# Expert layer of an audio tower: eight hidden buffers, products issued four experts at a time, and a new order of router and normalisation

## The chip, the cores and the metric

The kernel runs on one core of a Trainium2 chip. The time is that of one execution on the device, in microseconds (us).
## What is computed

The program is an audio tower of five blocks on 64 tiles of 128 tokens with 64 channels, in float32. The change touches the third block, the first layer of experts, a mixture of 16 experts in which each token uses the best two:

```python
gate_logits = x @ gate_w + gate_b
topk_vals, topk_idx = jax.lax.top_k(gate_logits, K)          # K = 2 of E = 16
topk_w = jax.nn.softmax(topk_vals, axis=-1)
h = jax.nn.relu(jnp.einsum('bsh,ehf->bsef', x, w1) + b1)     # 64 -> 128
expert_out = jnp.einsum('bsef,efh->bseh', h, w2) + b2        # 128 -> 64
sel = jnp.take_along_axis(expert_out, topk_idx[:, :, :, None], axis=2)
moe = jnp.sum(topk_w[..., None] * sel, axis=2)
y = x + moe
mu = jnp.mean(y, axis=-1, keepdims=True)
var = jnp.var(y, axis=-1, keepdims=True)
return (y - mu) / jnp.sqrt(var + EPS) * gamma + beta
```

Its x is the normalised output of the stage ahead, and its result is added to that output (`h`).

## The kernel before

`experts0` computes all 16 experts for every token and weighs the results, with weight 0 for the 14 that were not chosen. The tokens go in 16 groups (`TG`) of four tiles (512 tokens); two buffers `b` alternate. Two experts are a unit `n` (eight units, `NE`). Each engine has a program of its own for a group; nothing but the order written there and the semaphores sets the order of the work.

For a unit, TensorE's `hidden(n)` makes the 8 passes of the first product (L1320) into one of two pairs of PSUM banks (n even or odd); ScalarE applies a Relu for each of the two experts (L1496) into one of four buffers `hid`; TensorE's `out(n)` makes the 32 passes of the second product (L1332) into one of two banks; VectorE multiplies them with the tokens' weights into `part` (L1454); GpSimd adds `part` to the sum `acc` (L1282). `hidden(n)` must wait until the Relus of unit n-2 have read its banks. `Step.at(r, k)` is the value that a semaphore has after k events of round r.

Work for the next group g+1 is woven between the units of group g:

- the turn: GpSimd normalises g+1, TensorE transposes it (`T.pe`, L690), ScalarE copies it out (`T.act`, L697, into `xs`);
- the router: `logits` on TensorE (L1302), then on VectorE the logits (L1413), the best two by MAX8 and FIND_INDEX8, and the `gap` of the two (L1427); ScalarE takes its exponential (L1482), VectorE the two weights (`soften`), GpSimd the weights by expert (`weigh`);
- for the present group: TensorE transposes the weights (L1349), ScalarE copies them (`wT`, L1504), TensorE multiplies them with the experts' second biases (L1356), VectorE adds the input (`base`, L1461), and at the group's end `y` is the folded sum plus `base`.

The group before is normalised meanwhile (`finish`): statistics, variance, square root on ScalarE (L1489), and the result into `h`. Exp and Sqrt each need a table load on ScalarE, since they alternate. Groups 2 to 13 run in a hardware loop of two groups a turn, whose waits are computed in registers; groups 0, 1, 14 and 15 are written out. In the loop the table load for Exp stands behind the wait for `gap`; in the part written out it stands ahead of it.

In TensorE's order before, `hidden` runs one unit ahead: hidden(0), then for each n hidden(n+1), out(n). The turn of g+1 comes behind out(1), the logits of g+1 ahead of out(4). ScalarE does the turned copy behind the Relu of expert 7, Exp behind that of expert 13.

Of the kernel before, what the change touches and what calls it, by code (L numbers as in the profile page):

```python
# [17 lines left out]
ALU = mybir.AluOpType  # L18
# [4 lines left out]
C = 64  # L23
# [26 lines left out]
COLS += [("gatew", EXPERTS0), ("gatebr", EXPERTS0), ("iota16", EXPERTS0), ("eb1", EXPERTS0),  # L50
# [1129 lines left out]
def experts0(nc, ctx, m):  # L1180
# [18 lines left out]
    hid = [sb(f"hid{n}", [P, NT]) for n in range(4)]  # L1199
# [10 lines left out]
    yc_sb, yn_sb, h_sb, h_stat = step("yc_sb"), step("yn_sb", 2), step("h_sb"), step("h_stat", TS)  # L1210
# [9 lines left out]
    def rounds(eng, rest, ahead, finish=None):  # L1220

        def call(f, g, b):
            return lambda k: f(g, b, k) if f else None

        ahead(0, 0, None)
        rest(0, 0, call(ahead, 1, 1), call(None, 0, 0))
        rest(1, 1, call(ahead, 2, 0), call(finish, 0, 0))
        with eng.Fori(1, TG // 2 - 1) as i:
            rest(2 * i, 0, call(ahead, 2 * i + 1, 1), call(finish, 2 * i - 1, 1))  # L1230
            rest(2 * i + 1, 1, call(ahead, 2 * i + 2, 0), call(finish, 2 * i, 0))
        rest(TG - 2, 0, call(ahead, TG - 1, 1), call(finish, TG - 3, 1))
        rest(TG - 1, 1, call(None, 0, 0), call(finish, TG - 2, 0))
        for k in range(E if finish else 0):
            finish(TG - 1, 1, k)

    def pool(eng):
        def ahead(g, b, k):
            if k in (0, None):
                T.pool(eng, g, b)  # L1240

                sl = bass.ds(g * TS, TS)
                eng.wait_ge(T.norm_sb.sem, T.norm_sb.at(g, 1))
                settle(eng, m)
                eng.tensor_tensor(m.h[:, sl, :], m.h[:, sl, :], col(m, "betr").unsqueeze(1).broadcast_to([P, TS, C]),
                                  ALU.add).then_inc(beta_sb.sem, 1)

            if k in (1, None):
                weigh(g, b)

        def finish(g, b, k):

            if k == 3:
                sl = bass.ds(g * TS, TS)
                eng.wait_ge(var_sb.sem, var_sb.at(g))
                eng.wait_ge(yn_sb.sem, yn_sb.at(g - 1))
                settle(eng, m)
                eng.tensor_tensor(yc[:, :, :], m.y[:, sl, :], bc(y_mean[:, :], ALL), ALU.subtract).then_inc(yc_sb.sem, 1)
# [13 lines left out]
        def rest(g, b, ahead, finish):  # L1272
            for e in range(E):
                n = e // 2
                if e == 3:
                    eng.wait_ge(part_sb.sem, part_sb.at(g, 2))
                    eng.tensor_tensor(acc[:, :, :, :], part[0][:, :, :, :], part[1][:, :, :, :],
                                      ALU.add).then_inc(sum_sb.sem, 1)
                elif e % 2 and e > 1:
                    eng.wait_ge(part_sb.sem, part_sb.at(g, n + 1))  # L1280
                    eng.wait_ge(sum_sb.sem, sum_sb.at(g, n - 1))
                    eng.tensor_tensor(acc[:, :, :, :], acc[:, :, :, :], part[n % RING][:, :, :, :],  # L1282
                                      ALU.add).then_inc(sum_sb.sem, 1)
                finish(e)
                if e == 1:
                    ahead(0)
                if e == 14:
# [3 lines left out]
            eng.tensor_tensor(fold[:, :, :], acc[:, :, 0, :], acc[:, :, 1, :], ALU.add).then_inc(sum_sb.sem, 1)  # L1291

        eng.wait_ge(*T.norm)
        eng.memset(wT[:, :], 0.0).then_inc(zeros, 1)
        rounds(eng, rest, ahead, finish)

    def pe(eng):
        def logits(g, b):
            eng.wait_ge(T.xs_sb.sem, T.xs_sb.at(g))
            for p in range(TS // 2):  # L1300
                for r, rows in enumerate(HALVES):
                    mm = eng.matmul(m.ps[:, r, 256 + p * E:256 + (p + 1) * E], T.xs[b][rows, p * P:(p + 1) * P],  # L1302
                                    col(m, "gatew", rows), start=True, stop=True)
            mm.then_inc(logit_ps.sem, 1)

        def ahead(g, b, k):
            if k in (0, None):
                eng.wait_ge(logit_sb.sem, logit_sb.at(g - 1))
                T.pe(eng, g, b)
            if k in (1, None):  # L1310
                eng.wait_ge(base_sb.sem, base_sb.at(g - 1))
                logits(g, b)

        def rest(g, b, ahead, finish):
            def hidden(n):
                eng.wait_ge(hid_sb.sem, hid_sb.at(g, 2 * n - 2) if n >= 2 else hid_sb.at(g - 1))
                for j in range(2):
                    e = 2 * n + j
                    for r, rows in enumerate(HALVES):
                        mm = eng.matmul(m.ps[:, 2 + 2 * (n % 2) + r, j * 256:(j + 1) * 256],  # L1320
# [911 lines left out]
```

## Time and profile before

| what | value |
| --- | --- |
| median of 3 runs | 1213.65 us (1213.61 to 1213.88) |
| profiled execution | 1214.44 us, its span 1212.7 us, clock 0.939 |
| first to last product of this stage's experts | 422.6 to 786.4 us, with the norm behind it to 794.75 us |
| busy in the whole span | PE 1053.4, PEld 733.9, DVE 724.5, ACT 690.5, POOL 508.0 us |

A row of the time line gives the start (us from the span's start), the duration, the engine and line, what is written and read, how many instructions are merged in it, and in brackets how long the engine stood idle ahead of it and for whom. A row `x32` of L1332 is one unit's second product, `x8` of L1320 one unit's first product.

### The profile page before, as it was taken

The page shows a single profiled execution, that of the slowest core. Times are in us where ns is not written, and L with a number is a line of the kernel's source. Part 1 is how long each engine was busy: PE and PEld are TensorE (multiplying, and loading weights), DVE is VectorE, ACT ScalarE, POOL GpSimd, SP SyncE. Part 2 cuts the span into 40 slices and gives each one's busy share as a digit, 9 for nine tenths or more (in the row PEclk, how much of TensorE's full clock was granted, in tenths as well). Part 3 has the DMA queues.
Part 4 walks back from the last instruction along what each step waited for, and adds up shares of the span by engine and source line. Part 5 has one row for each costly group of instructions (what it writes and reads, how often), then busy time and mean ns, then how long its engine had stood idle before and what let it go on. Part 6 is the DMA issues. An engine that isn't in the chain of part 4 may idle for free.

```text
span 1212.7 us, 35394 instructions
## 1 busy us (share of the span) xinstructions
PE 1053.4 (87%) x12426; PEld 733.9 (61%) x12426; DVE 724.5 (60%) x1976; ACT 690.5 (57%) x1290; POOL 508.0 (42%) x780
## 2 busy tenths in 40 slices
PE   3698865999998798888888889969999999968998
PEld 1254444777766676666677667736666666645555
DVE  3466634677745646555655655627888888863443
ACT  1245443777754565565556556537777777744554
POOL 0000002555526455555555555534555555542110
PEclk9999986999977999899899989969999999988999
DMA  9423000000000000000000000000000000000101
GB/s 250 67 38 42 1 1 0 2 0 0 0 1 1 1 2 3 2 0 0 0 0 0 0 0 1 3 1 1 3 0 0 0 0 0 1 1 10 22 17 22
DMA packets 10769, 14.92 MB, mean 12 GB/s; under 512 B 9296, under 2 KB 9296, under 8 KB 9680
## 3 DMA queue, kind: packets, MB, share of 16 engines
q1 hardware_dynamic: 10704, 14.06, 5.5%
q8 instruction: 40, 0.66, 0.2%
q14 instruction: 25, 0.20, 0.1%
HBM read 11.96 MB, written 2.10 MB: 12 GB/s over the span
## 4 chain that ended last, share of the span: by engine, by line
PE 70%; DVE 10%; issue 10%; ACT 4%; POOL 4%; DVEq 1%; DMA 0%; ACTq 0%; SPq 0%; POOLq 0%
PE ps L1332 7%; PE ps L1320 7%; PE ps L1701 6%; PE ps L1723 5%; PE ps L1709 4%; PE ps L221 3%; PE ps L1691 3%; PE ps L1865 3%; PE ps L1898 3%; POOL e_acc L1282 3%; PE ps L1689 2%; PE ps L859 2%; PE ps L858 2%; PE ps L231 2%; DVE c_max L351 2%
## 5 line engine op out<-in xcount | busy, mean ns | idle before, releaser
L1496 ACT ACTIVATE e_hid<-ps,cst 128x512 f32<-128x512 f32 x256 | 161.3, 680 | 101.8 <-PE ps L1320 101.6
L1332 PE MATMUL ps<-ew,e_hid 128*64 128x64 f32 x4096 | 155.5, 230 | 41.1 <-ACT e_hid L1496 40.8
L1332 PEld LDWEIGHTS ps<-ew,e_hid 128*64 128x64 f32 x4096 | 136.2, 141 | 78.4 <-ACT e_hid L1496 48.3
L1282 POOL TENSOR_TENSOR e_acc<-e_acc,e_part 128x512 f32<-128x512 f32 x96 | 125.3, 1306 | 107.6 <-DVE e_part L1454 107.2
L1320 PE MATMUL ps<-e_xs,ew 64*128 64x256 f32 x1024 | 153.6, 428 | 0.0
L1454 DVE TENSOR_TENSOR e_part<-ps,e_wt 128x512 f32<-128x512 f32 x128 | 88.1, 688 | 99.0 <-PE ps L1332 95.9
L1320 PEld LDWEIGHTS ps<-e_xs,ew 64*128 64x128 f32 x1024 | 98.4, 204 | 19.7 <-issue 3.5
L1747 DVE TENSOR_REDUCE a_rmax<-ps 128x8 f32<-128x1024 f32 x64 | 78.2, 1223 | 36.0 <-PE ps L1701 34.0
L1656 POOL TENSOR_TENSOR a_sum<-a_part 128x256 f32<-128x256 f32 x64 | 46.5, 726 | 105.1 <-DVE a_part L1758 105.1
L1709 PEld LDWEIGHTS ps<-cst,a_ex 128*128 128x128 f32 x512 | 55.0, 140 | 49.7 <-issue 49.7
L204 POOL TENSOR_TENSOR t_prob<-t_ex,t_rscale 128x512 f32<-128x512 f32 x8 | 12.0, 1502 | 169.4 <-DVE t_rscale L377 169.4
L1750 DVE TENSOR_TENSOR a_diff<-ps,a_rmax 128x1024 f32<-128x1024 f32 x64 | 78.4, 1224 | 2.9
L1792 ACT ACTIVATE a_prob<-ps 128x1024 f32<-128x1024 f32 x64 | 65.6, 1024 | 20.3 <-PE ps L1709 18.7
L1701 PE MATMUL ps<-a_u,a_xs 64*128 64x512 f32 x256 | 71.5, 635 | 4.7 <-DVE a_diff L1750 4.5
L1723 PE MATMUL ps<-a_v,a_prob 128*64 128x66 f32 x2048 | 73.9, 224 | 1.1 <-DVE a_part L1758 1.1
L1723 PEld LDWEIGHTS ps<-a_v,a_prob 128*64 128x64 f32 x2048 | 65.0, 136 | 11.7 <-issue 11.7
L1709 PE MATMUL ps<-cst,a_ex 128*128 128x128 f32 x512 | 70.0, 279 | 1.7 <-ACT a_ex L1787 1.6
L221 PE MATMUL ps<-x_in,w1s 48*128 48x512 f32 x128 | 43.7, 764 | 31.1 <-DVE c_max L351 13.6
L351 DVE TENSOR_REDUCE c_max<-ps 128x128 f32<-128x1024 f32 x32 | 39.2, 1224 | 51.3 <-PE ps L221 51.3
L1787 ACT ACTIVATE a_ex<-a_diff 128x1024 f32<-128x1024 f32 x64 | 67.2, 1051 | 3.2 <-DVE a_diff L1750 2.6
L2000 ACT ACTIVATE e_hid<-ps,cst 128x512 f32<-128x512 f32 x64 | 38.8, 688 | 24.3 <-PE ps L1865 24.3
L1775 ACT ACTIVATE a_u<-ps 128x1024 f32<-128x1024 f32 x32 | 32.8, 1025 | 33.4 <-PE ps L1689 33.4
(272 smaller groups left out, 2207.4 us busy)
## 6 DMA issues: line engine op xcount, KB each, us to landing
x_in<-x_dram SPq DMA_DIRECT2D x48, 128.0 KB, 4.7
cst<-cst_dram SPq DMA_DIRECT2D x1, 2965.0 KB, 16.6
out_dram<-e_res SPq DMA_DIRECT2D x16, 128.0 KB, 2.0
ew<-ew_dram SPq DMA_DIRECT2D x1, 1024.0 KB, 18.6
cst<-cst_dram SPq DMA_DIRECT2D x1, 704.0 KB, 7.5
ew<-ew_dram SPq DMA_DIRECT2D x1, 512.0 KB, 20.3
cst<-cst_dram SPq DMA_DIRECT2D x1, 329.5 KB, 3.1
```

Of the source, the lines that this page charges most:

```text
L221: mm = eng.matmul(m.ps[:, r, :], w1s[rows, :], x_in[b][rows, h * 512:(h + 1) * 512], start=True, stop=True)
L1282: eng.tensor_tensor(acc[:, :, :, :], acc[:, :, :, :], part[n % RING][:, :, :, :], ALU.add).then_inc(sum_sb.sem, 1)
L1320: mm = eng.matmul(m.ps[:, 2 + 2 * (n % 2) + r, j * 256:(j + 1) * 256], w1[rows, e * F0:(e + 1) * F0], T.xs[b][rows, :], start=True, stop=True)
L1332: mm = eng.matmul(m.ps[rows, 6 + n % 2, to:to + C], hid[e % 4][:, a:a + C], w2[:, e * C:e * C + C], start=True, stop=True)
L1454: eng.tensor_tensor(part[n % RING][:, :, :, :], m.ps[:, 6 + n % 2, :].rearrange("p (s j c) -> p s j c", s=TS, j=2), wt[b][:, :, 2 * n:2 * ...
L1496: nc.scalar.activation(hid[e % 4][:, :].rearrange("p (r t) -> p r t", r=2), m.ps[:, 2 + 2 * (n % 2):4 + 2 * (n % 2), j * 256:(j + 1) * 256 ...
L1701: mm = eng.matmul(m.ps[:, 2 + h, :], T.xs[b][rows, s * P:(s + 1) * P], u[b][rows, s, :, :].rearrange("p h t -> p (h t)"), start=True, stop ...
L1709: mm = eng.transpose(m.ps[:, 4 + j // 4, (j % 4) * P:(j % 4 + 1) * P], ex[s % 2][:, j, :], col(m, "ident"))
L1723: mm = eng.matmul(m.ps[rows, 6 + j // 4, (j % 4) * P:(j % 4) * P + W], prob[s % 2][:, j, rows], v[b][:, s, head * V:head * V + W], start=T ...
L1747: eng.tensor_reduce(rmax[:, :], src, AX, ALU.max).then_inc(max_sb.sem, 1)
L1750: eng.tensor_tensor(diff[:, :, :], src, bc(rmax[:, :], [P, H, P]), ALU.subtract).then_inc(diff_sb.sem, 1)
L1787: nc.scalar.activation(ex[s % 2][:, :, :], diff[:, :, :], ACT.Exp).then_inc(exp_sb.sem, 1)
```

## The change

It changes the order on all four engines and a few sizes; the work is the same. TensorE issues the products of one kind for two units (four experts) in a row and runs two units ahead, into the next group: hidden(n+2), hidden(n+3), out(n), out(n+1). For this there are eight `hid` buffers. The turn of g+1 stands behind out(1) as before, the transposition of the weights now ahead of it; the logits of g+1 stand behind out(3), and are two products over all 128 rows (`gatebd`, 32 columns) where they were four over 64 rows. On ScalarE the turned copy and `wT` stand behind the Relu of expert 3, Exp behind that of expert 9, Sqrt behind that of expert 13. On VectorE the logits (`best`) stand ahead of the weighing of unit 2, the rest of the choice (`choose`) behind it, the gap ahead of the searches; the normalisation's steps are spread anew over two groups, and its product with gamma moves from VectorE to GpSimd (`scale`). GpSimd normalises two groups ahead. The core of the diff:

```diff
-    hid = [sb(f"hid{n}", [P, NT]) for n in range(4)]
+    hid = [sb(f"hid{n}", [P, NT]) for n in range(8)]
...
+        def rest(g, b, back, more):
+            if more:
+                beta(g + 1)
+            add(g, 1)
+            if back > 1:
+                scale(g - 2)
+            add(g, 2)
+            add(g, 3)
+            add(g, 4)
+            if back:
+                centre(g - 1)
+            add(g, 5)
+            if more > 1:
+                eng.wait_ge(base_sb.sem, base_sb.at(g))
+                T.pool(eng, g + 2, b)
+            add(g, 6)
+            if more:
+                weigh(g + 1, 1 - b)
+            add(g, 7)
...
-            hidden(0)
-            for n in range(NE):
-                if n + 1 < NE:
-                    hidden(n + 1)
-                if n == 4:
-                    ahead(1)
-                out(n)
-                if n == 1:
-
-                    ahead(0)
-                    eng.wait_ge(wt_sb.sem, wt_sb.at(g))
...
+        def turn(g, b):
+            eng.wait_ge(logit_sb.sem, logit_sb.at(g - 1))
+            T.pe(eng, g, b)
...
+                mm = eng.matmul(m.ps[:, 0, 256 + 2 * p * E:256 + 2 * (p + 1) * E], T.xs[b][:, p * P:(p + 1) * P],
+                                col(m, "gatebd"), start=True, stop=True)
...
+        def rest(g, b, back, more):
+            for k in range(0, NE, 2):
+                for n in (k + 2, k + 3):
+                    if n < NE:
+                        hidden(g, b, n)
+                    elif more:
+                        hidden(g + 1, 1 - b, n - NE)
+                out(g, b, k)
+                out(g, b, k + 1)
+                if k == 0:
+                    turn_weights(g, b)
+                    if more:
+                        turn(g + 1, 1 - b)
+                if k == 2:
+                    if more:
+                        logits(g + 1, 1 - b)
+                    biases(g)
...
+            for n in range(NE):
+                weighted(g, b, n)
+                if n == 0 and back > 1:
+                    normal(g - 2)
+                if n == 1:
+                    if back:
+                        sums(g - 1)
+                    if more:
+                        best(g + 1)
+                if n == 2:
+                    if more:
+                        choose(g + 1)
+                    if back:
+                        count_y(g - 1)
+                if n == 3:
+                    bias(g, b)
+                    if back:
+                        variance(g - 1)
+                if n == 4 and back > 1:
+                    result(g - 2)
+                if n == 5 and more:
+                    soften(g + 1)
+                if n == 6 and back > 1:
+                    count(g - 2)
...
+            eng.wait_ge(out_ps.sem, out_ps.at(g, n - 3) if n >= 4 else out_ps.at(g - 1, NE - 3 + n))
...
             for e in range(E):
+                relu(g, e)
+                if e == 3:
+                    if more:
+                        T.act(eng, g + 1, 1 - b, hid_ps)
+                    turned(g)
+                if e == 9 and more:
+                    exp(g + 1)
+                if e == 13 and back:
+                    deviation(g - 1)```

On ScalarE, in the loop's first group. Before, from the copy of the turned weights (L1504) on; L697 is the copy of the turned tokens:

```order
L1504 ACTIVATE e_wT<-ps 16x512
L1494 REGISTER_ALU
L1496 ACTIVATE e_hid<-ps,cst 128x512 x2
L695 REGISTER_ALU
L697 ACTIVATE e_xs<-ps 128x256
L1494 REGISTER_ALU
L1496 ACTIVATE e_hid<-ps,cst 128x512 x2
```

Now, from the Relus of unit 1 on (L1542 is the Relu, L1551 the copy of the weights):

```order
L1542 ACTIVATE e_hid<-ps,cst 128x512 x2
L695 REGISTER_ALU
L696 REGISTER_ALU
L697 ACTIVATE e_xs<-ps 128x256
L1547 REGISTER_ALU
L1548 REGISTER_ALU
L1551 ACTIVATE e_wT<-ps 16x512
L1540 REGISTER_ALU
L1541 REGISTER_ALU
L1542 ACTIVATE e_hid<-ps,cst 128x512 x2
```

Both copies have moved up ahead of the Relus of unit 2, and stand next to each other.

On TensorE, in the loop's first group, now, from the transposition of the weights (L1350) to the first products of units 4 and 5 (L1330) and the logits (L1319); L1342 is the second product, L690 the turn of the next group:

```order
L1350 MATMUL ps<-cst,e_wt 16x128 x4
L1313 REGISTER_ALU
L687 ISA
L688 REGISTER_ALU
L690 MATMUL ps<-cst,e_xn 128x128 x2
L1326 REGISTER_ALU
L1330 MATMUL ps<-e_xs,ew 128x256 x4
L1326 REGISTER_ALU
L1330 MATMUL ps<-e_xs,ew 128x256 x4
```

The turn now stands directly ahead of hidden(4); before, a turn at the same place was followed by hidden(3).

On VectorE, in the loop's first group. Before, from the weighing of unit 5 (L1454) to that of unit 6:

```order
L1454 TENSOR_TENSOR e_part<-ps,e_wt 128x512
L1412 REGISTER_ALU
L1413 TENSOR_TENSOR e_logit<-ps,cst 128x64
L1417 REGISTER_ALU
L1418 REGISTER_ALU
L1421 MAX e_top<-e_logit 128x8 x4
L1422 ISA
L1425 MAX_INDEX e_idx<-e_top,e_logit 128x8 x4
L1426 REGISTER_ALU
L1427 TENSOR_TENSOR e_gap<-e_top 128x4
```

Now, from `y` of the group before (L1394) to the gap (L1448); L1480 is the weighing of unit 2:

```order
L1394 TENSOR_TENSOR y<-e_fold,e_base 128x256
L1436 REGISTER_ALU
L1437 TENSOR_TENSOR e_logit<-ps,cst 128x64
L1439 REGISTER_ALU
L1442 MAX e_top<-e_logit 128x8 x4
L1477 REGISTER_ALU
L1480 TENSOR_TENSOR e_part<-ps,e_wt 128x512
L1445 ISA
L1447 REGISTER_ALU
L1448 TENSOR_TENSOR e_gap<-e_top 128x4
```

The logits are taken three units earlier, one weighing has come between them and the gap, and the four searches have gone behind the gap.

## Rows read from the trace of the kernel before

**Rows 1.** Waits in the stage: who waited for whom, us, times, longest

```profile
PE ps L1332 <- ACT e_hid L1496: 40.8, 22, 3.0
```

**Rows 2.** Time line, end of a group in the loop

```profile
576.00 0.21 DVE L1413 TENSOR_TENSOR e_logit<-ps,cst 128x64 f32<-128x64 f32 x1
...
576.44 0.41 DVE L1421 MAX8 e_top<-e_logit 128x8 f32<-128x16 f32 x4 [0.23 <-DVE e_logit L1413]
...
577.59 0.15 DVE L1427 TENSOR_TENSOR e_gap<-e_top 128x4 f32<-128x4 f32 x1
...
577.84 1.28 ACT L1482 ACT_TABLE_LOAD   x1 [2.48 <-DVE e_gap L1427]
...
579.25 1.25 ACT L1496 ACTIVATE e_hid<-ps,cst 128x512 f32<-128x512 f32 x2
...
579.97 1.97 PE L1332 MATMUL ps<-ew,e_hid 128*64 128x64 f32 x32 [2.69 <-ACT e_hid L1496]
```

**Rows 3.** Bases' line L1461: whole stage, then the loop's groups 2 to 13

```profile
L1461 DVE TENSOR_TENSOR e_base<-ps,e_xn x16: 416/419/419, 435.3 to 779.8; 128x256 f32<-128x256 f32 x16
...
L1461 DVE TENSOR_TENSOR e_base<-ps,e_xn x12: 416/419/419, 477.1 to 736.3; 128x256 f32<-128x256 f32 x12
```

**Rows 4.** Time line, TensorE's pieces at full clock in one group

```profile
587.67 0.44 PE L690 MATMUL ps<-cst,e_xn 128*128 128x128 f32 x2
...
588.48 1.13 PE L1320 MATMUL ps<-e_xs,ew 64*128 64x256 f32 x8
...
593.09 0.64 PE L1356 MATMUL ps<-cst,e_wT 128*64 128x64 f32 x16
...
594.80 0.62 PE L1302 MATMUL ps<-cst,e_xs 64*128 64x16 f32 x8
...
595.35 1.15 PE L1332 MATMUL ps<-ew,e_hid 128*64 128x64 f32 x32
...
596.43 1.14 PE L1320 MATMUL ps<-e_xs,ew 64*128 64x256 f32 x8
```

**Rows 5.** Time line of TensorE: a seam at full clock, two first products in a row

```profile
556.60 1.26 PE L1332 MATMUL ps<-ew,e_hid 128*64 128x64 f32 x32 [2.69 <-ACT e_hid L1496]
557.79 2.00 PE L1320 MATMUL ps<-e_xs,ew 64*128 64x256 f32 x16
559.81 1.26 PE L1332 MATMUL ps<-ew,e_hid 128*64 128x64 f32 x32
```

**Rows 6.** Time line, end of the stage: two second products in a row, last statistics

```profile
784.53 2.12 PE L1332 MATMUL ps<-ew,e_hid 128*64 128x64 f32 x64
...
794.15 0.60 DVE L496 BATCH_NORM_STATS2 stat<-h 128x6 f32<-128x64 f32 x4 [0.15 <-DVE h L1404]
```

**Rows 7.** Time line of ScalarE: its two copies

```profile
590.28 0.57 ACT L1504 ACTIVATE e_wT<-ps 16x512 f32<-16x512 f32 x1
...
591.90 0.36 ACT L697 ACTIVATE e_xs<-ps 128x256 f32<-128x256 f32 x1
```

**Rows 8.** Costliest groups: the weighing on VectorE

```profile
L1454 DVE TENSOR_TENSOR e_part<-ps,e_wt 128x512 f32<-128x512 f32 x128 | 88.1, 688 | 99.0 <-PE ps L1332 95.9 <-issue 2.5
```

**Rows 9.** Time line of TensorE: first and last of the loop's twelve seams

```profile
486.32 1.29 PE L1332 MATMUL ps<-ew,e_hid 128*64 128x64 f32 x32 [2.69 <-ACT e_hid L1496]
...
491.07 1.15 PE L1332 MATMUL ps<-ew,e_hid 128*64 128x64 f32 x32
...
745.50 1.26 PE L1332 MATMUL ps<-ew,e_hid 128*64 128x64 f32 x32 [2.68 <-ACT e_hid L1496]
```

**Rows 10.** By stretches: busy us of PE, PEld, DVE, ACT, POOL, then PEclk

```profile
488.00:492.00 4.00, 4.00 (x47) 3.01 (x46) 1.55 (x4) 2.07 (x4) 3.04 (x5) 0.65 0.01 2
556.00:560.00 4.00, 3.38 (x54) 2.75 (x56) 2.48 (x8) 2.06 (x4) 2.98 (x5) 1.00 0.00 0
```

**Rows 11.** Time line of a group written out: table load, and TensorE's wait

```profile
460.11 1.28 ACT L1482 ACT_TABLE_LOAD   x1
...
463.36 0.82 PE L1332 MATMUL ps<-ew,e_hid 128*64 128x64 f32 x20 [1.36 <-ACT e_hid L1496]
```

More of the change, by code:

```diff
@@ L1218, in experts0 @@
     ALL = [P, TS, C]
[L1220 to L1228, printed above, removed]
-        with eng.Fori(1, TG // 2 - 1) as i:
[L1230 to L1235, printed above, removed]
@@ L1237, in pool, with rounds @@
-    def pool(eng):
[L1238 to L1258, printed above, removed]
+    def rounds(eng, rest, tail=None):
+        rest(0, 0, 0, 2)
+        rest(1, 1, 1, 2)
+        with eng.Fori(1, TG // 2 - 1) as i:
+            rest(2 * i, 0, 2, 2)
+            rest(2 * i + 1, 1, 2, 2)
+        rest(TG - 2, 0, 2, 1)
+        rest(TG - 1, 1, 2, 0)
+        if tail:
+            tail(TG - 1, 1)
@@ new lines, in logits, with hidden @@
+                mm = eng.matmul(m.ps[:, 0, 256 + 2 * p * E:256 + 2 * (p + 1) * E], T.xs[b][:, p * P:(p + 1) * P],
+                                col(m, "gatebd"), start=True, stop=True)
+            mm.then_inc(logit_ps.sem, 1)
+        def hidden(g, b, n):
+            if n == 0:
+                eng.wait_ge(T.xs_sb.sem, T.xs_sb.at(g))
+            eng.wait_ge(hid_sb.sem, hid_sb.at(g, 2 * n - 2) if n >= 2 else hid_sb.at(g - 1, E - 2 + 2 * n))
+            for j in range(2):
+                e = 2 * n + j
+                for r, rows in enumerate(HALVES):
+                    mm = eng.matmul(m.ps[:, 2 + 2 * (n % 2) + r, j * 256:(j + 1) * 256],
+                                    w1[rows, e * F0:(e + 1) * F0], T.xs[b][rows, :], start=True, stop=True)
+            mm.then_inc(hid_ps.sem, 1)
@@ new lines, in out @@
+        def out(g, b, n):
+            eng.wait_ge(part_sb.sem, part_sb.at(g, n - 1) if n >= 2 else part_sb.at(g - 1, NE - 1 + n))
+            for j in range(2):
+                e = 2 * n + j
+                eng.wait_ge(hid_sb.sem, hid_sb.at(g, e + 1))
+                for s in range(TS):
+                    for rows in HALVES:
+                        a, to = place(s) * P + rows.start, (2 * s + j) * C
+                        mm = eng.matmul(m.ps[rows, 6 + n % 2, to:to + C], hid[e % 8][:, a:a + C],
+                                        w2[:, e * C:e * C + C], start=True, stop=True)
+            mm.then_inc(out_ps.sem, 1)
@@ new lines, in rest @@
+        def rest(g, b, back, more):
+            for n in range(NE):
+                weighted(g, b, n)
+                if n == 0 and back > 1:
+                    normal(g - 2)
+                if n == 1:
+                    if back:
[17 more added lines that the diff above has]
+                    count(g - 2)
@@ L1511, in act @@
         eng.preload_act_table(ACT.Exp)
-        rounds(eng, rest, ahead, finish)
+        T.act(eng, 0, 0, hid_ps)
+        exp(0)
+        rounds(eng, rest, tail)
     return dict(pool=pool, pe=pe, dve=dve, act=act)
@@ L2201, in more_constants @@
     rows("bm2r", a0("b2"))
-    twice("gatew", f0("gate_w")), rows("gatebr", f0("gate_b"))
+    for s in range(2):
+        gate = np.zeros((C, 2, EXPERTS0), np.float32)
+        gate[:, s, :] = f0("gate_w")
+        put("gatebd", gate, 64 * s)
+    rows("gatebr", f0("gate_b"))
     rows("iota16", np.arange(EXPERTS0, dtype=np.float32))
```

320 lines of the change are left out of this document (151 added, 169 removed).

## The prediction

> **What bounds the kernel now.** I read the waits of the stage first, then a time line of one group in the loop, then TensorE's rows and the clock. TensorE is the engine that is nearly always busy here, and what it waits for is ScalarE's Relus [rows 1]. The time line shows where: at the end of a group VectorE takes the logits (576.00), finds the gap, and only then may ScalarE load its table (577.84) and take the exponential; the last unit's Relus stand behind that, so TensorE stands idle for 2.69 us, until 579.97 [rows 2]. This happens in each of the loop's twelve groups, with waits of 2.68 to 2.96 us [rows 9]. The shorter waits for the same line make up the rest of the 40.8 us in 22 times [rows 1].
>
> The period of a group in the loop follows from the bases' first and last row: (736.3 - 477.1) / 11 = 23.56 us. The four other periods are 344.5 - 259.2 = 85.3 us, 21.3 on average [rows 3]; one reason is that there the table load runs ahead of the wait, and TensorE waits 1.36 us [rows 11].
>
> The clock belongs to it. The first seam is followed by a stretch at a clock of 0.65, so mostly at 1.2 GHz; the seam at 556.60 is followed by 1.00 [rows 10]. Stretches of four us over the whole stage show such a fall behind ten of the twelve seams, and none behind the stage's waits of 1.36 us or less. Its price is in TensorE's rows: from the end of the wait to the next-but-one piece it takes 491.07 - 486.32 = 4.75 us with the fall, and 559.81 - 556.60 = 3.21 without it [rows 5, 9]. That is 1.54 us here. Where one group's piece alone can be compared, 1.97 against 1.26 us [rows 2, 5], at least 0.7 was lost. I take 1.45, near the first, since it compares the whole stretch.
>
> **TensorE's work in the new order.** A row's end lies 0.07 us behind the next piece's start (595.35 + 1.15 against 596.43) [rows 4]. One unit's second product takes 1.08, its first 1.07 [rows 4]. Two first products in a row take 559.81 - 557.79 = 2.02 [rows 5], two second ones 2.12 - 0.07 = 2.05 [rows 6]. A group of four such blocks is 4 x 4.07 = 16.28 us. The turn and the transposition of the weights are 588.48 - 587.67 = 0.81, the bias products 0.57, the logits 0.55 [rows 4]. For the new logits, four passes over 128 rows instead of eight over 64, no row exists: the turn's two passes bound them from below (0.28), the old logits' row from above (0.62). I take 0.55, since each pass loads weights for the whole array. Sum: 18.21 us. The old order was 16 x 1.075 - 0.12 (one pair in a row already) + 1.93 = 19.0, so the grouping is worth 0.8 us a group, some 13 us in the stage, if nothing waits.
>
> **Wait A, behind the turn.** On TensorE the turn of g+1 now stands directly ahead of hidden(4), and hidden(4) needs the Relus of unit 2. On ScalarE those stand behind the copy of the turned tokens, which needs the turn. ScalarE cannot work ahead: it stands idle from the Relus of unit 1, through out(0) and out(1), and then does in a row the turned copy (0.36) and `wT` (0.57) [rows 7], and two Relus (1.25) [rows 2]. With about 0.2 for the turn's own tail and the handovers, less 0.1 of overlap, TensorE waits 2.3 us; hidden(5) wants two more Relus and waits another 0.1. In the old order the copy stood behind the Relu of expert 7 and had two units' time, so nothing of this was on the path. A = 2.4 us. VectorE and the sums are idle meanwhile, and nothing else is late first.
>
> **Wait B, behind the logits.** hidden(7) needs the Relus of unit 5, and these stand on ScalarE behind Exp, which needs the gap. The logits come behind out(3). From their end: handover 0.1; logits and MAX8 576.00 to 576.85, 0.85 [rows 2]; the weighing of unit 2, which now lies between, 0.69 [rows 8]; waits 0.1; the gap 0.15; handover 0.1; table load and Exp 577.84 to 579.25, 1.41; two Relus 1.25 and a handover 0.04 [rows 2]. Sum 4.7 us, less about 0.1 of overlap. TensorE has meanwhile the bias products and hidden(6), 0.57 + 1.07 = 1.64 [rows 4]. B = 2.9 us. The eight buffers do not help in either case: what hidden(n) waits for is its pair of banks, not `hid`.
>
> Here the Trainium skill (ScalarE: Activation LUTs, What ACT_TABLE_LOAD costs) says otherwise on the switch: beside the load of 1283 ns it counts a drain of some 1380 ns. The row of the load agrees with the first number, but the Relus start at 579.25, 0.13 us behind the load's end with Exp between them, so there is no such drain here [rows 2]. By the page B would be 4.3 us, and the time of the sum below 12 x 1.38 = 17 us longer.
>
> **The sum.** Without falls of the clock a group in the loop takes 18.21 + 2.4 + 2.9 = 23.5 us, against 23.56 measured with the old falls. So the 13 us of grouping, and the seam's old wait, are given back in two new waits. To this come the falls. B is as long as the old seam's waits, of which 10 in 12 led to a fall; A is a little shorter, and lies between those and the 1.36 us that led to none, nearer to the first. I take 0.85 and 0.6 falls: 1.45 x 1.45 = 2.1 us a group. After both waits TensorE's work is what everything waits for, so I let them count in full. Loop: (23.5 + 2.1 - 23.56) x 12 = +24.5 us.
>
> Outside the loop A is the same and B 1.28 shorter, since the load runs ahead: 18.2 + 2.4 + 1.6 = 22.2 us, against 21.3. With the last group, which has no A-like wait now, I count +5 for the four. Behind the last products there were 794.75 - 786.65 = 8.1 us [rows 6]; now two groups' normalisation is left there instead of one, and the product with gamma goes to GpSimd and back: +3. Falls behind A in these four groups: 4 x 0.6 x 1.45 = +3.5. Sum: 24.5 + 5 + 3 + 3.5 = +36 us. VectorE and GpSimd lose and gain 0.4 to 0.6 us a group by the move of gamma, which their idle time hides: VectorE stands idle ahead of the logits while wait A, a block's first pair and its second pair go by on TensorE, 2.4 + 2.0 + 2.05, an estimate of 6 us. If that cover were gone it would be 0.5 x 16 = 8 us. The wider column `gatebd` is nothing.
>
> The sum is made against the profiled execution, 1214.4 us, which lies 0.8 above the median; against the median it gives 1249.6. I predict **1250 us**.
>
> **Rivals.**
>
> *The clock holds.* A and B stay at full clock. Then the loop is 23.5 against 23.56, the outside +8: 1213.65 - 1 + 8 = 1221 us. With falls behind B alone (10 in 12) it is 1221 + 12 x 1.2 = 1236. The Trainium skill (TensorE: Matmul & The Clock Gate, Why this matters for your kernels) asks only that longer idle gaps than either of these be avoided, which is this case. Against it: ten falls behind waits of the same size as B. For it: A is shorter than any wait that led to one. 0.21 for 1216 to 1236.
>
> *Faster.* One of the two waits isn't there, because ScalarE's copy or Exp finds its input earlier than I say. It decides at 23.56 - 18.21 - 8/12 = 4.7 us of waits and falls a group; below that the kernel is faster. With B and its falls alone, 18.2 + 2.9 + 1.2 = 22.3 us: -15 in the loop, 1206 with the outside. With neither it would be 18.2 us and some 64 less in the loop, 1157, which is the change doing what its grouping offers. Against both: the orders on TensorE, ScalarE and VectorE tie the waits into rings that no earlier work can open, and the pieces are all rows. 0.06.
>
> *No change.* The clock holds, and the ends cost nothing: 0.02.
>
> *Worse.* Both waits lead to a fall every time, at 1.54 us: (23.5 + 3.1 - 23.56) x 12 + 8 + 6 = +51, 1265; with the page's drain 1267 even with my falls. Beyond 1264: 0.05.
>
> **How the numbers follow.** My own case, 1236 to 1264, has 0.66; the clock case 0.21, faster 0.06, the same 0.02, worse 0.05. The range 1220 to 1264 takes in the first two, but for the lowest part of the second. Faster by over 0.2% (about what a measurement of this kernel tells from none) 0.06, within it 0.03, slower 0.91.
>
> **What would show it.** Right: TensorE's two waits per group are for `hid` at the first product's line, of 2.3 to 2.5 and 2.7 to 3.1 us, where before they were at the second's; ScalarE waits some 5 us per group for the turn and 3 or more for the gap; VectorE waits 6 us for the logits; the loop's period is 25 to 26 us; the mean clock of the stage is lower; pairs of pieces take 2.02 and 2.05. Wrong: a period under 23.5 us, a wait of TensorE for `part` or for GpSimd, or a clock of 1.00 behind most waits.

## The result

The changed kernel takes 1248.2 us in the median of four runs (1244.94 to 1252.73) against 1213.77 us for the kernel before, run beside it: a ratio of 1.0277, with an interval of 1.0232 to 1.0323. It is slower by 2.8%, about 34 us. The profiled execution took 1252.73 us, its span is 1250.9 us, and its mean clock 0.921 against 0.939.

The page's first part, after. The engines do the same work, and PE's busy time is only longer because more of its work ran at the lower clock:

```profile
PE 1060.8 (85%) x12362; PEld 743.4 (59%) x12362; DVE 721.6 (58%) x1960; ACT 685.2 (55%) x1288; POOL 515.8 (41%) x796
```

The waits of the stage, after (who waited for whom: us in all, times, longest):

```profile
POOL e_acc L1272 <- DVE e_part L1480: 170.4, 49, 8.7
DVE e_logit L1437 <- PE ps L1319: 106.4, 16, 8.4
ACT e_xs L697 <- PE ps L690: 78.4, 16, 5.4
PE ps L1330 <- ACT e_hid L1542: 70.1, 34, 2.6
ACT L1531 <- DVE e_gap L1448: 53.8, 12, 5.6
```

TensorE's wait for the Relus was 40.8 us in 22 times at the second product's line [rows 1]; it is now 70.1 us in 34 times, and at the first product's line. ScalarE waits 4.9 us a group for the turn (78.4 / 16) and 4.5 for the gap (53.8 / 12, the loop's groups), VectorE 6.7 for the logits (106.4 / 16).

The time line, after, of one group in the loop. Its first rows are the seam behind the turn (wait A), then comes the seam behind the logits (wait B):

```profile
556.08 0.38 PE L690 MATMUL ps<-cst,e_xn 128*128 128x128 f32 x2
...
556.50 0.38 ACT L697 ACTIVATE e_xs<-ps 128x256 f32<-128x256 f32 x1 [5.15 <-PE ps L690]
...
556.78 0.57 ACT L1551 ACTIVATE e_wT<-ps 16x512 f32<-16x512 f32 x1
...
557.25 3.73 ACT L1542 ACTIVATE e_hid<-ps,cst 128x512 f32<-128x512 f32 x6
...
558.54 2.27 PE L1330 MATMUL ps<-e_xs,ew 64*128 64x256 f32 x16 [2.08 <-ACT e_hid L1542]
...
560.74 2.08 PE L1342 MATMUL ps<-ew,e_hid 128*64 128x64 f32 x64
...
562.76 0.63 PE L1319 MATMUL ps<-cst,e_xs 128*128 128x32 f32 x4
...
563.43 0.23 DVE L1437 TENSOR_TENSOR e_logit<-ps,cst 128x64 f32<-128x64 f32 x1 [6.28 <-PE ps L1319]
563.80 0.41 DVE L1442 MAX8 e_top<-e_logit 128x8 f32<-128x16 f32 x4
...
564.12 0.67 DVE L1480 TENSOR_TENSOR e_part<-ps,e_wt 128x512 f32<-128x512 f32 x1
564.71 0.15 DVE L1448 TENSOR_TENSOR e_gap<-e_top 128x4 f32<-128x4 f32 x1
...
564.96 1.28 ACT L1531 ACT_TABLE_LOAD   x1 [3.98 <-DVE e_gap L1448]
...
566.37 2.40 ACT L1542 ACTIVATE e_hid<-ps,cst 128x512 f32<-128x512 f32 x4
...
567.67 1.81 PE L1330 MATMUL ps<-e_xs,ew 64*128 64x256 f32 x8 [2.60 <-ACT e_hid L1542]
...
568.07 1.26 POOL L1272 TENSOR_TENSOR e_acc<-e_acc,e_part 128x512 f32<-128x512 f32 x1 [1.85 <-DVE e_part L1480]
568.24 1.12 DVE L1403 TENSOR_TENSOR e_y_diff<-stat 128x4 f32 x1
...
569.41 2.97 PE L1342 MATMUL ps<-ew,e_hid 128*64 128x64 f32 x64
...
569.73 0.16 DVE L1412 SCALAR_TENSOR_TENSOR e_y_var<-e_y_m,e_y_dd 128x4 f32<-128x4 f32 x1
569.99 1.28 ACT L1536 ACT_TABLE_LOAD   x1 [1.22 <-DVE e_y_var L1412]
...
571.49 1.25 ACT L1542 ACTIVATE e_hid<-ps,cst 128x512 f32<-128x512 f32 x2
...
572.31 2.00 PE L1330 MATMUL ps<-e_xs,ew 64*128 64x256 f32 x16
...
574.24 2.09 PE L1342 MATMUL ps<-ew,e_hid 128*64 128x64 f32 x64
```

Where before one seam held TensorE for 2.69 us [rows 2], there are two, of 2.08 and 2.60 us. ScalarE's chains are those of the prediction: turn, both copies, two Relus; gap, table, exponential, two Relus. The pair of first products behind A takes 560.74 - 558.54 = 2.20 us, where an undisturbed pair takes 1.93 (574.24 - 572.31): its second half waits 0.27 us for two more Relus, which the row hides. The rows from 568.07 on show a third chain that isn't in the prediction: a variance that comes late, its table load for Sqrt, and two Relus (571.49) behind it. I call it C.

By stretches of four us, after (busy us of PE, PEld, DVE, ACT, POOL, then PEclk). The stretch behind A's seam is at full speed here, the one behind B's is near 1.2 GHz:

```profile
560.00:564.00 4.00, 4.00 (x94) 3.47 (x90) 0.43 (x4) 0.99 (x2) 0.00 (x0) 1.00 0.00 0
...
568.00:572.00 4.00, 4.00 (x66) 3.27 (x64) 2.43 (x8) 2.77 (x5) 1.26 (x1) 0.57 0.00 0
```

Over the whole loop the clock fell behind all twelve of B's seams, and behind five of the twelve of A's (those that end at 482.04, 532.46, 607.54, 684.26 and 709.93). One with its fall, and what follows it:

```profile
482.04 3.23 PE L1330 MATMUL ps<-e_xs,ew 64*128 64x256 f32 x16 [2.16 <-ACT e_hid L1542]
...
487.59 0.63 PE L1319 MATMUL ps<-cst,e_xs 128*128 128x32 f32 x4
```

The bases' line, after, whole stage:

```profile
L1471 DVE TENSOR_TENSOR e_base<-ps,e_xn x16: 414/415/416, 445.0 to 815.1; 128x256 f32<-128x256 f32 x16
```

The loop's groups 2 to 13 take their bases from 492.75 to 770.01, a period of 25.21 us against 23.56 [rows 3]. The profiled execution's 38.2 us more of span divide so: 9.7 ahead of the first base (445.0 against 435.3), 18.1 in the loop's eleven intervals, 7.5 in the other four, 2.9 behind the last base. Of the 9.7, 1.0 us already stands ahead of the stage (its first turn starts at 421.59 against 420.61).

### The profile page after: what moved, and what is told of

The parts are those of the page before. It is cut to its first block, busy times and chain, and to the rows that moved or that the text cites. A ratio compares the mean times of both kernels' runs of the same rounds, so it can differ in the third digit from the quotient of the medians.

```text
span 1250.9 us, 35285 instructions
## 1 busy us (share of the span) xinstructions
PE 1060.8 (85%) x12362; PEld 743.4 (59%) x12362; DVE 721.6 (58%) x1960; ACT 685.2 (55%) x1288; POOL 515.8 (41%) x796
## 4 chain that ended last, share of the span: by engine, by line
PE 75%; DVE 9%; issue 6%; ACT 6%; POOL 1%; ACTq 0%; DMA 0%; SPq 0%; DVEq 0%; POOLq 0%
PE ps L1342 11%; PE ps L1330 10%; PE ps L1760 5%; PE ps L1782 4%; PE ps L1768 4%; ACT e_hid L1542 3%; PE ps L221 3%; PE ps L1750 3%; PE ps L1924 3%; PE ps L1957 2%; PE ps L1748 2%; PE ps L231 2%; PE ps L859 2%; PE ps L858 2%; DVE c_max L351 2%
## 5 line engine op out<-in xcount | busy, mean ns | idle before, releaser
L1330 PE MATMUL ps<-e_xs,ew 64*128 64x256 f32 x1024 | 154.9, 438 | 70.1 <-ACT e_hid L1542 70.1
L1272 POOL TENSOR_TENSOR e_acc<-e_acc,e_part 128x512 f32<-128x512 f32 x96 | 123.3, 1284 | 171.0 <-DVE e_part L1480 170.4
L1542 ACT ACTIVATE e_hid<-ps,cst 128x512 f32<-128x512 f32 x256 | 155.5, 677 | 21.1 <-PE ps L1330 19.8
L1330 PEld LDWEIGHTS ps<-e_xs,ew 64*128 64x128 f32 x1024 | 100.8, 206 | 100.3 <-ACT e_hid L1542 87.1
L1342 PEld LDWEIGHTS ps<-ew,e_hid 128*64 128x64 f32 x4096 | 141.0, 153 | 26.5 <-issue 15.3
L1342 PE MATMUL ps<-ew,e_hid 128*64 128x64 f32 x4096 | 149.8, 238 | 0.0
L1480 DVE TENSOR_TENSOR e_part<-ps,e_wt 128x512 f32<-128x512 f32 x128 | 87.8, 686 | 81.4 <-PE ps L1342 78.7
L1809 DVE TENSOR_TENSOR a_diff<-ps,a_rmax 128x1024 f32<-128x1024 f32 x64 | 78.4, 1225 | 7.5 <-DVE a_rmax L1806 1.7
L1437 DVE TENSOR_TENSOR e_logit<-ps,cst 128x64 f32<-128x64 f32 x16 | 3.6, 225 | 106.4 <-PE ps L1319 106.4
L697 ACT ACTIVATE e_xs<-ps 128x256 f32<-128x256 f32 x32 | 12.5, 390 | 83.5 <-PE ps L690 83.5
```

The costliest lines, as they stand in the source:

```text
L1342: mm = eng.matmul(m.ps[rows, 6 + n % 2, to:to + C], hid[e % 8][:, a:a + C], w2[:, e * C:e * C + C], start=True, stop=True)
L1480: eng.tensor_tensor(part[n % RING][:, :, :, :], m.ps[:, 6 + n % 2, :].rearrange("p (s j c) -> p s j c", s=TS, j=2), wt[b][:, :, 2 * n:2 * ...
L1542: nc.scalar.activation(hid[e % 8][:, :].rearrange("p (r t) -> p r t", r=2), m.ps[:, 2 + 2 * (n % 2):4 + 2 * (n % 2), j * 256:(j + 1) * 256 ...
L1809: eng.tensor_tensor(diff[:, :, :], src, bc(rmax[:, :], [P, H, P]), ALU.subtract).then_inc(diff_sb.sem, 1)
```

## The experiments

All are edits of the changed kernel, unless said otherwise, and each ratio is against the kernel before on the same chip. At 1213.8 us, 0.1% is 1.2 us; a ratio is known to within 0.2 to 0.3% (the changed kernel's to within 0.5%), so a difference of two of them is known to some 3 to 6 us. The loop's periods come from the bases' starts, as above.

### One wait removed at a time, and both

**The copies later (A away).** ScalarE makes both copies behind the Relu of expert 7, where the turned tokens' copy stood before the change, and not behind that of expert 3. The copy of the weights now comes first of the two:

```diff
-                if e == 3:
-                    if more:
-                        T.act(eng, g + 1, 1 - b, hid_ps)
+                if e == 7:
                     turned(g)
+                if e == 7 and more:
+                    T.act(eng, g + 1, 1 - b, hid_ps)
```

> The changed kernel, with ScalarE's two copies (turned tokens and turned weights) behind the Relu of expert 7 instead of expert 3. Theory (two rings, A through the turned copy, B through Exp): wait A of 2.1 us is gone, B of 2.6 us stays at the first product of unit 7; the loop's period falls from 25.3 to 20.8 us without falls of the clock and to 22 with one behind most of B's waits; about 1197 us. Rival (the waits only move: hidden(4) then waits for something else, or B grows by what A loses): 1235 us or more. Rival (the ring A did not cost more than its own 2.1 us, and falls stay as many): 1215 us.

Measured: 1198.96 us, ratio 0.9848 (0.9829 to 0.9866), the loop's period 22.25 us. TensorE waits 40.5 us in 22 times, nearly the old number. No wait stands behind the turn any more; most of it is B. In the loop the clock fell behind eight of the twelve B's. In the four groups without a fall, and only in those, a further wait of 0.92 us comes behind B, at the place of C:

```profile
502.15 1.13 PE L1330 MATMUL ps<-e_xs,ew 64*128 64x256 f32 x8 [2.61 <-ACT e_hid L1542]
...
507.28 1.14 PE L1330 MATMUL ps<-e_xs,ew 64*128 64x256 f32 x8 [0.92 <-ACT e_hid L1542]
```

So A with its falls costs 4.3%, net of the C that comes out here, and this one place already makes the kernel faster than before.

**The tables later (B away, and C with it).** Exp behind the Relu of expert 11 and Sqrt behind that of 15; the copies stay behind the Relu of expert 3, but this edit too puts the copy of the weights first:

```diff
                 if e == 3:
-                    if more:
-                        T.act(eng, g + 1, 1 - b, hid_ps)
                     turned(g)
-                if e == 9 and more:
+                if e == 3 and more:
+                    T.act(eng, g + 1, 1 - b, hid_ps)
+                if e == 11 and more:
                     exp(g + 1)
-                if e == 13 and back:
+                if e == 15 and back:
                     deviation(g - 1)
```

> The changed kernel, with Exp behind the Relu of expert 11 instead of 9, and Sqrt behind expert 15 instead of 13; the copies stay behind expert 3. Theory: wait B is gone, A of 2.1 us stays; period 20.8 us without falls, 21.7 with falls behind half of A's waits; about 1196 us. Rival (Exp is late wherever it stands, so the same 2.6 us appear two units later, at the next group's first product): 1240 us.

Measured: 1213.33 us, ratio 0.9977 (0.9958 to 0.9995), 17 us above the number expected. TensorE's waits in this kernel:

```profile
PE ps L1330 <- ACT e_hid L1542: 30.6, 17, 1.9
PE ps L1342 <- DVE e_part L1480: 15.3, 15, 1.1
...
PE ps L1350 <- POOL e_wt L1263: 5.0, 13, 0.4
```

B is gone and A remains, once in each group (1.9 us each in the loop). That is 0.1 to 0.3 us less than in the changed kernel; the weights' copy now starts before the turn has ended. Two waits that I had not reckoned with have appeared, together 20 us: the second product for VectorE's weighing (which stands behind the logits and searches there), and the turned weights for GpSimd.

**Both.** Copies behind expert 7, Exp behind 11, Sqrt behind 15:

> The changed kernel with both moves: the copies behind expert 7, Exp behind 11, Sqrt behind 15. Theory: neither ring is closed, TensorE waits under 1 us a group, the clock stays at 1.00 in the stage, the period is its work, 18.5 to 19 us; about 1157 us, faster than both kernels by 5%. Rival (a third wait takes the place of the two: VectorE's weighing, late by the router's work, holds back the second products): period 20.5 us, 1178 us.

Measured: 1163.05 us, ratio 0.9550 (0.9531 to 0.9570), the loop's period 19.51 us and the clock 1.00 throughout the loop. Its waits of TensorE:

```profile
PE ps L1342 <- DVE e_part L1480: 15.2, 15, 1.1
PE ps L1350 <- POOL e_wt L1263: 5.1, 13, 0.4
```

In the middle of the groups no wait for a Relu is left. Less these two waits, TensorE's own work is 19.51 - 1.1 - 0.4 = 18.0 us a group, where the prediction had 18.21. So the new order of products is good by itself: A, B and C (Sqrt has moved too), with the falls, are worth more than all of what was lost.

### What the falls of the clock cost

Here TensorE fills both seams with idle products, six in each, that is 12 passes, into a bank that nobody reads at that time. In the rows below the passes end 0.8 to 1.1 us before the Relus do, so that nothing comes later for them.

```diff
+        def fill(g, n, passes):
+            eng.wait_ge(part_sb.sem, part_sb.at(g, n - 1))
+            for _ in range(passes):
+                eng.matmul(m.ps[:, 6, 0:P], col(m, "ident"), col(m, "ident"), start=True, stop=True)
...
+                    if n == 7:
+                        fill(g, 4, 6)
...
                         turn(g + 1, 1 - b)
+                    fill(g, 2, 6)
```

> The changed kernel with idle work on TensorE in both waits: six products of the unit matrix with itself, 12 passes and an estimated 1.5 us, behind the turn and again ahead of hidden(7), written to a bank that is free there and never read. Nothing else moves. It tells the clock's part from the waits' part. Theory (each wait costs its length, and a fall of the clock behind it as much as its slow passes lose): the rings keep their length, so the period without falls is 23.3 us as it would be, but the clock stays at 1.00; the time falls by all of the falls' cost, 20 to 26 us, to about 1224 us. Rival (falls cost little, since other waits absorb them, and the order alone made the kernel slower): 1245 us. Rival (the added passes delay the products behind them): over 1250 us.

Measured: 1235.06 us, ratio 1.0148 (1.0124 to 1.0173). The whole loop by stretches, first of the changed kernel, then of this one (the same columns as above):

```profile
484.00:724.00 240.00, 194.88 (x3262) 159.21 (x3262) 127.45 (x454) 125.78 (x207) 124.38 (x146) 0.89 0.00 0
```

```profile
484.00:724.00 240.00, 212.25 (x3654) 175.69 (x3652) 130.83 (x465) 133.42 (x220) 135.51 (x160) 1.00 0.00 0
```

The clock stays at 1.00, and the time falls by 1.3% (15.7 us, uncertain by some 6), not by the 2.0% expected. The falls are a real cost and smaller than I had made them. This kernel's time line shows why (idle products are L1315, first products L1335, Exp's table load L1539, Sqrt's L1544):

```profile
557.41 1.61 PE L1315 MATMUL ps<-cst 128*128 128x128 f32 x12
560.08 1.14 PE L1335 MATMUL ps<-e_xs,ew 64*128 64x256 f32 x8 [1.06 <-ACT e_hid L1550]
...
562.42 1.28 ACT L1544 ACT_TABLE_LOAD   x1 [1.23 <-DVE e_y_var L1420]
...
563.92 2.40 ACT L1550 ACTIVATE e_hid<-ps,cst 128x512 f32<-128x512 f32 x4
...
565.22 1.14 PE L1335 MATMUL ps<-e_xs,ew 64*128 64x256 f32 x8 [0.92 <-ACT e_hid L1550]
566.28 2.09 PE L1347 MATMUL ps<-ew,e_hid 128*64 128x64 f32 x64
...
572.90 1.50 PE L1315 MATMUL ps<-cst 128*128 128x128 f32 x12
575.22 2.27 PE L1335 MATMUL ps<-e_xs,ew 64*128 64x256 f32 x16 [0.82 <-ACT e_hid L1550]
577.42 2.09 PE L1347 MATMUL ps<-ew,e_hid 128*64 128x64 f32 x64
...
579.44 0.63 PE L1324 MATMUL ps<-cst,e_xs 128*128 128x32 f32 x4
```

Filled, the seams end at the same distance as unfilled: the first products ahead of the idle ones end at 557.49, and from there to 560.08 it is 2.59 us, as B is 2.60 unfilled. But at 565.22 TensorE meets a third wait, of 0.92 us: C. In the changed kernel there is none at that place in the loop, since TensorE comes there late at the low clock. From the end of wait B to the second products behind the next pair of first ones takes 566.28 - 560.08 = 6.20 us here, and 574.24 - 567.67 = 6.57 us there. So this fall behind B costs 0.4 us and not the 1.5 that its own pieces lose, because it covers C. Eleven of the twelve cost 0.2 to 0.4 us so; behind the B that ends at 667.41 the clock stayed low longer, and that one costs 1.7. Behind A nothing covers a fall: from 482.04 to 487.59, 5.55 us, against 579.44 - 575.22 = 4.22 at full clock. The five falls behind A cost 1.3 to 1.6 us each, 1.46 on average.

**The third wait.** The same with Sqrt moved behind the last Relu:

```diff
-                if e == 13 and back:
+                if e == 15 and back:
                     deviation(g - 1)
```

> The kernel with idle passes in the two waits (clock at 1.00 all through), and Sqrt moved from behind the Relu of expert 13 to behind that of 15, nothing else. In that trace a third wait of 0.9 us a group stands at the next group's hidden(1), which the prediction did not have. Theory: it comes from Sqrt, whose variance VectorE gives late, ahead of the Relus of unit 7; it goes, and the period falls from 24.2 to 23.3 us: 11 to 14 us less than with the passes alone, about 1223 us. Rival (Exp's four Relus are what is late, and the wait only moves on): 1235 us.

Measured: 1219.28 us, ratio 1.0035 (1.0019 to 1.0052). This is 1.1% (13.7 us) below the one with the fill alone, and the loop's period falls from 24.23 to 23.04 us. TensorE's wait for the Relus falls from 36.7 us in 42 times to 25.3 in 29: thirteen waits less, twelve of them C in the loop's groups. So C comes from Sqrt's place, and costs 1.2 us a group once the clock holds: the wait of 0.92, and the rest because it splits a pair of first products. What it costs in the changed kernel, where the falls behind B cover it, was not run; had C been taken out there first, the falls behind B would probably have cost more.

**The kernel before, filled.** The same idle products in the old order, 16 passes in the loop's one seam:

> The kernel before, with idle work on TensorE in the seam of the loop's twelve groups: eight products of the unit matrix with itself, 16 passes and an estimated 2.1 us of the 2.7 us wait, written to a bank that is free there. It tells what the old falls of the clock cost. Theory: the shorter wait behind Sqrt (0 to 1.2 us) takes up most of an old fall, so the falls cost 0.3 to 0.5 us each, and the kernel gains 3 to 5 us. Rival (a fall costs the 1.45 us that its slow passes lose, as the prediction charged for the new ones): 12 to 15 us faster.

Measured: 1210.0 us, ratio 0.9960 (0.9944 to 0.9975). Its stretch over the loop has a clock of 1.00 where the kernel before has 0.94:

```profile
484.00:724.00 240.00, 219.84 (x3750) 178.43 (x3752) 140.11 (x498) 139.87 (x227) 134.49 (x157) 1.00 0.00 0
```

So its ten falls cost 4.9 us together by the ratio (3.0 to 6.8 by its interval), some 0.5 each, and the loop's period goes from 23.56 to 23.33 only, 2.8 us over twelve groups. The 1.54 us that I had read from [rows 5, 9] is what a fall takes from its own pieces; most of it comes back at a later wait. In the kernel before, a wait of 1.2 us stands behind each of the two seams without a fall (at 543.55 and 566.91), and behind the ten with one it is 0.5 us or none.

### What the eight buffers do

Four buffers, and the Relu's wait for the second product with them:

```diff
-    hid = [sb(f"hid{n}", [P, NT]) for n in range(8)]
+    hid = [sb(f"hid{n}", [P, NT]) for n in range(4)]
...
-            eng.wait_ge(out_ps.sem, out_ps.at(g, n - 3) if n >= 4 else out_ps.at(g - 1, NE - 3 + n))
+            eng.wait_ge(out_ps.sem, out_ps.at(g, n - 1) if n >= 2 else out_ps.at(g - 1, NE - 1 + n))
```

> The changed kernel with four hidden buffers instead of eight; a Relu then waits until the second product of the unit two before has read its buffer. Order unchanged. Theory as the prediction has it (what hidden(n) waits for is its banks, so buffers are not what waits A and B are about): both stay, but with the order of four experts in a row the Relus of units n+2 and n+3 now can't run under the first products, and a new wait of 1 to 2 us a block comes on top: 1260 to 1275 us. Rival (eight buffers do nothing): 1248 us. Rival (the eight buffers are what makes the change slow): under 1240 us.

Measured: 1290.8 us, ratio 1.0621 (1.0586 to 1.0656), above the range that I had given. From its waits:

```profile
ACT e_hid L1542 <- PE ps L1342: 138.8, 47, 4.1
...
PE ps L1330 <- ACT e_hid L1542: 102.0, 71, 2.6
```

ScalarE now waits for second products, three times a group, and TensorE waits for ScalarE twice as often as with eight. A and B themselves are what they were (2.08 and 2.60 us). With both sets of moves from above, and four buffers:

> The kernel with copies and both table functions late (1163 us), with four hidden buffers. Theory: with four experts in a row the Relus of units n+2 and n+3 need buffers of their own under the products; with four they wait for the second products and hidden(n+4) waits for them, 0.5 to 1 us a block at its first product: 1175 to 1195 us. Rival (once no ring is closed the Relus have time enough): 1163 us.

Measured: 1181.34 us, ratio 0.9731 (0.9712 to 0.9749), 1.8% above the same order with eight. The buffers are thus no help against A and B, and a condition for the grouping.

### What the grouping is worth

The order with both moves, but with the products one unit at a time (hidden(k+2), out(k), hidden(k+3), out(k+1)):

```diff
-                for n in (k + 2, k + 3):
+                for j in range(2):
+                    n = k + j + 2
...
-                out(g, b, k)
-                out(g, b, k + 1)
+                    out(g, b, k + j)
```

> The kernel with copies and both table functions late (1163 us), with TensorE's products in turns of one unit (hidden(n+2), out(n), hidden(n+3), out(n+1)), still two units ahead. It measures what four experts in a row are worth once nothing waits. Theory: two changes of kind more a block at 0.10 to 0.13 us, 0.5 to 0.8 us a group: 8 to 13 us slower, about 1173 us. Rival (the turns give VectorE an earlier start on each unit, so its 1.1 us wait a group goes and pays for it): 1158 to 1163 us.

Measured: 1179.12 us, ratio 0.9689 (0.9659 to 0.9719). Against the grouped order's 0.9550 the grouping is worth 1.4%, 17 us; the prediction's sum had 13 for it "if nothing waits". Some 2.5 of the 17 are waits for the weighings, 17.7 us here against 15.2.

### The version that came out of it

Both moves, and on VectorE the logits behind the weighing of unit 2 and no longer ahead of it, so that the weighing for which TensorE waits comes first:

```diff
-                if n == 1:
-                    if back:
-                        sums(g - 1)
-                    if more:
-                        best(g + 1)
+                if n == 1 and back:
+                    sums(g - 1)
                 if n == 2:
                     if more:
+                        best(g + 1)
                         choose(g + 1)
```

> The kernel with copies and both table functions late (1163 us), and on VectorE the logits taken behind the weighing of unit 2 instead of ahead of it. Theory: VectorE no longer stands before the logits with a finished unit unweighed, so TensorE's wait of 1.1 us a group for the parts is gone: period 18.1 to 18.4 us, about 1150 us. Rival (the gap comes later, Exp and the weights too, and the wait for the weights at the group's start, 0.4 us now, grows): 1163 us.

Measured: 1150.2 us, ratio 0.9465 (0.9441 to 0.9489), 5.3% faster than the kernel before, the loop's period 18.71 us. Its waits of TensorE for other engines in the middle of groups:

```profile
PE ps L1350 <- POOL e_wt L1263: 5.2, 13, 0.4
...
PE ps L1342 <- DVE e_part L1480: 1.9, 7, 0.7
```

The wait for the weighings is 1.9 us where it was 15.2. With 18.0 us of work in a period of 18.71, TensorE's own work is now nearly all that the stage takes.

## Why the prediction was right

**The waits.** Both came where it had them and at the line that it named. The rows show 2.08 to 2.16 us for A and 2.60 for B in the loop, both a little under the bounds that the prediction set as signs (2.3 to 2.5, 2.7 to 3.1). The same two chains set them: each move took its wait away (ratio 1.0277 to 0.9848 without A, 0.9977 without B and C, 0.9550 without all three). A's sum was right: the second wait, for which it had 0.1, is 0.27 inside the pair's row, so A is 2.35 to 2.43 against 2.4. B is 0.3 shorter, since from the end of the logits' products (563.32) to hidden(7) (567.67) it takes 4.35 us and not 4.6, and TensorE has 1.74 us of work meanwhile and not 1.64. ScalarE's idle time for the turn is 4.9 us (5 predicted), for the gap 4.5 (3 or more), VectorE's for the logits 6.7 (6).

**TensorE's work.** Pairs of first products take 1.93 to 2.00 us and of second ones 2.01 (2.02 and 2.05 predicted), the new logits 563.32 - 562.76 = 0.56 (0.55). The filled kernel without C checks the sum: 23.04 - 2.12 - 0.27 - 2.60 = 18.05 us a group, and the kernel without the waits gives 18.0; 18.21 was predicted.

**The loop's period.** Without falls I had 23.5 us, and the measurement is 23.04 without C and 24.23 with it. With the falls 25.6 was predicted and 25.21 measured. The prediction's 18.21 + 2.4 + 2.9 for a group leaves C out, 1.2 us, and is 0.5 too long in what it has. "After both waits TensorE's work is what everything waits for, so I let them count in full" is right behind A and wrong behind B: 1.45 falls a group at 1.45 us were 2.1 us, and measured they come to 25.21 - 24.23 = 0.98 us. Their number was right in sum, 17 behind the loop's 24 seams where 17.4 were predicted, but not in its parts: 5 of 12 behind A (0.6 predicted) and 12 of 12 behind B (0.85). The price was right behind A (1.46 us), while behind B the slow pieces cover C and eleven of the twelve cost 0.2 to 0.4.

**Over the whole kernel**, by differences of ratios times 1213.8: the change costs 33.6 us, of which the falls are 15.7 (28.7 in the prediction, if its terms are counted from none: 12 x 2.1 + 3.5; the kernel before had 4.9 of its own), C 13.7, and the rest 4.2. Each is uncertain by some 2 to 6 us, and the division holds in this order only, falls first and then C. The forecast of +36 is close because a wait that was missing makes up for falls that were priced too high and a sum of work and waits that was 0.5 us a group too long. That is luck. The mechanism was right; the closeness of 1250 to 1248 is better than its terms deserved.

**The time behind and around the loop.** Predicted were +5 and +3 with +3.5 of falls, 11.5 us in all. In the profiled execution the loop's twelve periods are 19.8 us longer, and the 18.4 us that are left of its 38.2 lie outside. The last products end at 816.78 + 4.03 = 820.8, 430.1 us ahead of the end, where it was 426.0 [rows 6]: 4.1 against the 3 predicted. Most of the rest stands ahead of the first base, 9.7 us; 1.0 us of it was there ahead of the stage, and then the first group runs into A with a fall behind it (a piece of 3.67 us in place of 2.27), and its base stands behind one more pair of first products. That this is its cause was not tried apart. Outside the loop the clock fell behind all three A's, where the prediction had 0.6 for each. The last group, to which the prediction gave no wait like A, waits 1.81 us at the same line, for the Relus behind the copy of its weights, with a fall behind it.

**The rivals.** "The clock holds" (1221 to 1236) was the one to take seriously, and the seventeen falls decide against it. The Trainium skill (TensorE: Matmul & The Clock Gate, Why this matters for your kernels) tolerates gaps of this length; behind the loop's waits of 2.08 to 2.62 us the clock went to 1.2 GHz 17 times in 24 here, and behind one of 1.81 us in the last group, so the measurement stands against it. The drain that the Trainium skill counts beside a table load (ScalarE: Activation LUTs, What ACT_TABLE_LOAD costs) isn't there either: in the filled kernel the load for Sqrt ends at 563.70 and the Relus start at 563.92, with the square root in between.

**The change's purpose.** "The eight buffers do not help in either case" holds for the two waits. As a judgement on the change it would be wrong: the changed order is 4.5% faster than the kernel before once ScalarE's four steps (two copies, Exp, Sqrt) stand a few units later, and 5.3% with one of VectorE's. Of that, 1.8% is lost with four buffers and 1.4% without the grouping; what the other parts of the change give was not tried apart.

## What to carry to other kernels

When products are grouped, every small step of another engine that stands between two groups' Relus must be looked at again: it has to stand where its input is already there, or else the engine that was to be kept busy waits for it. Price a fall of the clock by filling its seam with idle products, not by the slow pieces alone. If another wait follows, it gives back most of what these lose (0.2 to 0.4 us was left behind B, some 0.5 in the kernel before); if none does, the fall costs all of it (1.46 us behind A). The fill itself is a cheap gain (0.4% and 1.3% here). And look for the next wait behind the one that you remove: C came out only where the clock held, and the wait for the weighings only with B gone.

## What the hardware showed beside

**A tiny operation of VectorE stretched by GpSimd.** The difference of the variances (L1403), 128x4 elements, takes 1118 ns in the changed kernel in the median, where it took 155. First after, then before (min/median/max of its duration in ns, first and last start):

```profile
L1403 DVE TENSOR_TENSOR e_y_diff<-stat x16: 155/1118/1128, 468.8 to 827.8; 128x4 f32 x12, 128x4 f32<-128x4 f32 x4
```

```profile
L1378 DVE TENSOR_TENSOR e_y_diff<-stat x16: 153/155/165, 449.7 to 791.1; 128x4 f32 x12, 128x4 f32<-128x4 f32 x4
```

It starts at 568.24 while GpSimd's addition (568.07, 1.26 us) runs, and ends at 569.36, 0.03 us behind the end of that; in the filled kernel it is the same, 1.12 us beside an addition. This is what the Trainium skill says of the two engines (SBUF — State Buffer, 🔬 SBUF: two separate sides): an operation of VectorE with two inputs in SBUF is blocked by one of GpSimd's that reads SBUF and started first, for as long as that lasts. The stretch is 0.97 us, and C's wait 0.92. The copy of the found indices (L1452) shows the same sign: 0.75 us where it took 0.17 before, and it ends at 566.24, 0.03 us behind GpSimd's addition of 564.95. VectorE is busy without a gap from there to the variance, so both delay it. So the new order's C is probably these collisions: without them the load for Sqrt would start 1 to 1.5 us earlier. That is argued from the rows; a run with the variance moved clear of the addition wasn't made.

**Table loads.** A load takes 1.28 us. In the loop, where the waits are computed in registers, it stands behind the wait for the gap, and B is 2.60 us there; in the groups written out it runs ahead of the wait, and B is 1.24 to 1.49.
